# A graph network kernel: node rows sent in source order to runs of four slots, and summed from linear loads

## The reference

```python
def layer(x, conv):  return x + conv(relu(layernorm(x)))
# layer 0: Gaussian mixture; msg = einsum(xg[src], gauss(edge_attr)); mean over dst
# layer 1: SAGE mean, twice
h = relu(mean_over_dst(x[src]) @ W1_l + b1 + x @ W1_r)
out = mean_over_dst(h[src]) @ W2_l + b2 + h @ W2_r
# layer 2: spline convolutions on edge coordinates; summed over src (row = src, col = dst)
h = elu(spline_conv(ones)); h = elu(spline_conv(h)); h = elu(h @ w3 + b3)
t = h @ w4 + b4
new_pseudo = clip(pseudo + t[col] - t[row], 0, 1)
out = spline_conv(x, new_pseudo, conv_w)
# layer 3: SAGE with a sum instead of the mean, twice
```

## Time and profile before

| what | us |
|---|---|
| median of 3 runs | 15050.08 |
| fastest and slowest run | 15047.9, 15058.99 |
| the profiled execution's own time | 15074.62 |
| its span | 15072.8 |
| POOL busy in the span | 8971.3 |
| PE busy | 7096.2 |
| DVE busy | 5575.7 |
| ACT busy | 1755.8 |

### The profile page before, as it was taken

The page is one execution under the profiler, slowest core; times in us unless marked ns, Lnnn a source line. Parts: engine busy times, 40 slices in busy tenths (PEclk is TensorE's granted clock), DMA queues, the critical chain, the costliest instruction groups (busy, mean ns, idle before and its releaser), DMA issues. The chain is left out here.

```text
span 15072.8 us, 155974 instructions
## 1 busy us (share of the span) xinstructions
PE 7096.2 (47%) x32816; PEld 6021.4 (40%) x32819; DVE 5575.7 (37%) x11340; ACT 1755.8 (12%) x5296; POOL 8971.3 (60%) x9011
## 2 busy tenths in 40 slices
PE   5200455556665555455557775444444453334333
PEld 1100344446663333344446664433333343333332
DVE  8200344444445666333335554333233341111111
ACT  0000333322221111000010001111111110000000
POOL 0677566636665555555526665666666526664666
PEclk9555666655557777555555555555555555555555
DMA  7991111123331111211121112000111121112112
GB/s 271 139 106 13 53 67 67 64 70 91 89 86 34 42 41 40 26 30 31 30 13 12 12 12 15 12 12 12 21 23 23 24 34 12 12 12 12 13 13 14
DMA packets 790129, 641.91 MB, mean 43 GB/s; under 512 B 363646, under 2 KB 680304, under 8 KB 789814
## 3 DMA queue, kind: packets, MB, share of 16 engines
q1 hardware_dynamic: 466548, 303.70, 11.4%
q0 software_dynamic: 295168, 243.14, 9.1%
q10 hardware_dynamic: 28288, 93.72, 1.6%
HBM read 264.86 MB, written 386.20 MB: 43 GB/s over the span
## 5 line engine op out<-in xcount | busy, mean ns | idle before, releaser
L802 PE MATMUL ps<-got,oh 128*128 128x33 f32 x7040 | 1670.1, 400 | 2383.0 <-DVE oh L625 675.8
L802 PEld LDWEIGHTS ps<-got,oh 128*128 128x128 f32 x7040 | 1573.8, 327 | 2547.0 <-issue 2531.9
L765 POOL DMA_INDIRECT got<-q_table,idx x1760 | 1809.7, 1028 | 1186.1 <-DVE idx L807 657.2
L2144 POOL DMA_INDIRECT msg<-msg,idx x1792 | 1759.0, 982 | 1126.1 <-issue 524.4
L765 POOL DMA_INDIRECT got<-h_table,idx x1760 | 1719.1, 977 | 1116.8 <-issue 569.9
L1703 POOL DMA_INDIRECT cell<-rec,idx x880 | 921.6, 1047 | 609.4 <-ACT rec L1685 352.1
L348 POOL DMA_INDIRECT rec_r<-sc_rec,sc_idx x832 | 840.8, 1011 | 721.3 <-ACT sc_rec L339 423.2
L1367 POOL DMA_INDIRECT rec_d<-rec,idx x880 | 908.6, 1032 | 563.6 <-ACT rec L1307 310.5
L1969 POOL DMA_INDIRECT cell<-rec,idx x880 | 912.9, 1037 | 498.7 <-issue 270.8
L625 DVE TENSOR_TENSOR oh<-iota_f,rd 128x512 f32<-128x512 f32 x1105 | 759.7, 692 | 1025.1 <-DMA b<-in_L_gnn_b 498.2
L807 DVE CAST idx<-rd 128x4 int32 (+1 forms) x892 | 158.1, 178 | 2441.6 <-DMA msg<-msg,idx 634.8
(11 more groups left out here) (329 smaller groups left out, 13359.1 us busy)
## 6 DMA issues: line engine op xcount, KB each, us to landing
got<-rec_d SPq DMA_DIRECT2D x220, 416.0 KB
rec_d<-padd ACTq DMA_DIRECT2D x4, 11648.0 KB
rec_d<-padd ACTq DMA_DIRECT2D x4, 11232.0 KB
cin<-cell SPq DMA_DIRECT2D x224, 136.0 KB
msg<-msg,idx POOLq DMA_INDIRECT x1792
msg<-zpad SPq DMA_DIRECT2D x8, 3575.0 KB
got<-msg SPq DMA_DIRECT2D x220, 130.0 KB
cell<-rec,idx POOLq DMA_INDIRECT x1760
```

The costliest lines, as they stand in the source:

```text
L765: nc.gpsimd.indirect_dma_start(out=s["got"][:, n, g, :], out_offset=None, in_=table, in_offset=bass.IndirectOffsetOnAxis(ap=s["idx"][:, n, ...
L802: mm = nc.tensor.matmul(psum_rows[:, ds(at[g], W)], s["oh"][:, n, g, :], s["got"][:, n, g, 0:W], start=False, stop=False)
L2144: nc.gpsimd.indirect_dma_start(out=msgs, out_offset=bass.IndirectOffsetOnAxis(ap=idx[:, n, g:g + 1], axis=0), in_=msg[:, n, g, :], in_offs ...
```

## The change

The destination order is laid out anew. Inside a destination block edges are now sorted by source block as well, and the edges of one source block and one destination block take whole runs of RUN = 4 slots, the last one padded. That makes 944 tiles (236 batches, 59 turns of 4), of which the destination pass goes over 936 in turns of UBD = 6 batches instead of UB = 10. The "d" sort leaves the first phase; a new phase `place_by_runs` reads the source-ordered records back and makes the places from counts by block pairs.

With that, one source block's rows for a run are 4 x 128-lane picks. `send_runs` (four times) goes over 272 sets of 128 runs in source order: DVE compares the runs' local numbers with the lane (bf16), PE picks the rows in four bf16 matmuls from `planes`, in which a row's f32 values stand as three bf16 parts (HW = 100 values a slot; TW = 112 with t), ACT copies the result to `rec`, and POOL sends it with one indirect DMA, 128 runs of 800 B (896 B with t) to their places in run_h or run_t. `job_sum_runs` (four times) then loads 512 slots a batch linearly (SP), and PE adds them with twelve bf16 matmuls. Once, `source_runs` makes the runs' places and local numbers by way of DRAM, `job_send_ids` sends them in 236 indirect DMAs of 12 B beside `job_sum_out`, which now runs without a gather beside it, and `turn_ids` reads them back.

Tables: rec_d has 944 tiles. SP's fills in the scatter phase are now cell1 and msg1 alone; cell2 and msg2 are filled by ACT beside `job_sum_out`, waited for one by one. run_h and run_t are filled by ACT at the start of the source pass, sixteen issues in a row (`together=True`), and waited for at its end. h_table and q_table are gone, and so are most tick increments on PE, ACT and DVE. `to_cells` goes over 944 tiles.

```diff
-                    sort_sp(sp, srt["d"], "d", "d")
-                    sort_pe(pe, srt["d"], 50)
-                    parts, groups = 8, TILES_N // 4
+                    parts, groups = 8, TILES_D // 4
...
+        def blank_tables(eng, sem, tables, together=False):
+            parts, filled = 8, 0
+            for table, pad, tiles in tables:
+                groups = tiles // 2
...
+                for q in range(parts):
+                    t0, t1 = groups * q // parts, groups * (q + 1) // parts
+                    eng.dma_start(view[:, t0:t1, :], bcast(pad.unsqueeze(1), [P, t1 - t0, pad.shape[1]])).then_inc(sem, 16)
+                    filled += 16
+                    if not together:
+                        eng.wait_ge(sem, filled)
...
+        row_d = sb_in(early, "row_d", [P, TILES_N])
+        place_by_runs(row_d)
...
+                        blanks = blank_tables(act, s_blank, ((run_h, zpad[:, 0:HW], TILES_D), (run_t, zpad[:, 0:TW], TILES_D)), True)
                         act.wait_ge(s_const, 6)
                         act.wait_ge(s_ld[0], 16)
                         ramps(0, 0)
...
+        def send_runs(planes, W, runs):
+            RING = 4
...
+                                sp.dma_start(loc[:, u, :, :].rearrange("p b e -> p (b e)"),
+                                             bcast(loc_s[ds((i * UNROLL + u * HU) * RUN * P, HU * RUN * P)].unsqueeze(0),
+                                                   [P, HU * RUN * P])).then_inc(s_ld[u], 16)
...
+                                v.wait_ge(s_pick, k + 1)
+                                nc.vector.tensor_scalar(hot[:, m % RING, :], loc[:, u, m % HU, :], lane_c[:, 0:1], None,
+                                                        ALU.is_equal).then_inc(s_hot, 1)
...
+                                for g in range(RUN):
+                                    mm = nc.tensor.matmul(ps[:, m % RING, g * W:(g + 1) * W], hot[:, m % RING, g * P:(g + 1) * P],
+                                                          flat[:, ds(ids[m % HU] * W, W)], start=True, stop=True)
...
+                                act.wait_ge(s_pick, k + 1 + RING)
+                                nc.scalar.copy(rec[:, m, :].bitcast(BF16), ps[:, m % RING, 0:RUN * W]).then_inc(s_fill, 1)
...
+                                nc.gpsimd.indirect_dma_start(
+                                    out=out, out_offset=bass.IndirectOffsetOnAxis(ap=idx[:, u, m % HU:m % HU + 1], axis=0),
+                                    in_=rec[:, m, :], in_offset=None,
...
-        def job_sum_in_rows(c, table, width, acc, t_nm=None, new=None):
+        def job_sum_runs(c, runs, W, acc, planes=None, new=None):
...
+                        sp.wait_ge(free, i * R + n + 1)
+                        sp.dma_start(got[:, n, :, :], view[:, ds(i * STEP + n * G, G), :]).then_inc(loaded[n], 16)
...
                 for g in range(G):
-                    mm = nc.tensor.matmul(psum_rows[:, ds(at[g], W)], s["oh"][:, n, g, :], s["got"][:, n, g, 0:W],
-                                          start=False, stop=False)
+                    for q in range(3):
+                        mm = nc.tensor.matmul(psum_rows[:, ds(at[g], AW)], s["oh"][:, n, g, :], part_of[n][:, g, q * AW:(q + 1) * AW],
+                                              start=False, stop=False)
...
+                nc.vector.tensor_reduce(there[:, n % 2, :, :],
+                                        part_of[n][:, :, 3 * AW:3 * AW + 12].rearrange("p g (q f) -> p g f q", q=3)[:, :, 0:KD, :],
+                                        AX.X, ALU.add).then_inc(s_there, 1)
...
+                source_runs(pay, idx)
...
-                    run_sums(job_sum_in_rows(e, h_table, C + 1, acc_nm), job_sum_out(e, msg1, F1, acc_s[:, :]))
+                    run_sums(job_sum_out(e, msg1, F1, acc_s[:, :]),
+                             job_send_ids(pay, idx, sem_in(e, "sent"), ((cell2, pad2[:, :, :].rearrange("p u w -> p (u w)"), TC),
+                                                                        (msg2, zpad[:, 0:2 * (F2 + 1)], TILES_N)), sem_in(e, "blanked")),
+                             count=NI)
+                turn_ids()
...
+            send_runs(planes, HW, run_h)
+                run_sums(job_sum_runs(d, run_h, HW, acc_nm))
...
+            send_runs(planes_t, TW, run_t)
-                run_sums(job_sum_in_rows(d, q_table, QW, acc_nm, t_nm[:, :], new))
+                run_sums(job_sum_runs(d, run_t, TW, acc_nm, planes_t, new))
```

More of the change, by code:

```diff
@@ L49 @@
 ABANKS2 = -(-NB // PER_BANK2)
[L50 to L51 removed]
+MQ = 8
+MAPLEN = MQ * P
+assert max(TILES_C, TILES_N, TILES_D, SSETS) <= MAPLEN
 KS, KD = 5, 3
@@ L178, in halves_of, with count_bins @@
             return t.rearrange("p (h j) -> p h j", h=2)
-        def sort_dve(v, then, c, key, bins, blocks, tiles, row_out, tag):
+        def count_bins(v, c, key, bins):
             marks = c["marks"]
@@ L199, in sort_dve, with carry_bases @@
             then(nc.vector.tensor_scalar(c["first"][:, :], c["first"][:, :], float(P), None, ALU.mult))
-            then(nc.vector.scalar_tensor_tensor(out=seen[:, :], in0=seen[:, :], scalar=c["first"][:, 0:1], in1=total[:, :],
-                                                op0=ALU.add, op1=ALU.subtract))
+        def carry_bases(then, c):
+            seen, pos, lane = c["seen"], c["pos"], c["lane"]
             then(nc.vector.tensor_copy(pos[:, :], seen[:, :]))
@@ L205, in sort_dve, with keep_ranks @@
             nc.vector.tensor_copy(c["parts"][:, :], lane[:, :]).then_inc(c["carried"], 1)
+        def keep_ranks(v, then, c, key, bins, tiles, row_out):
+            marks, rank, pos, lane, half = c["marks"], c["rank"], c["pos"], c["lane"], c["rank"].shape[1] // 2
             def keep(b):
@@ L225, in sort_dve, with sum_columns, count_pe @@
                                                 op0=ALU.mult, op1=ALU.add))
+        def sum_columns(then, c):
+            total, seen = c["total"], c["seen"]
+            cols = total.shape[1]
+            then(nc.vector.tensor_copy(halves_of(total[:, :]), ps[:, 0:2, 0:cols // 2]))
+            then(nc.vector.tensor_tensor_scan(out=seen[:, :], data0=bcast(ones[:, 0:1], [P, cols]), data1=total[:, :],
+                                              initial=0.0, op0=ALU.mult, op1=ALU.add))
+        def sort_dve(v, then, c, key, bins, blocks, tiles, row_out, tag):
+            count_bins(v, c, key, bins)
+            total, seen = c["total"], c["seen"]
+            sum_columns(then, c)
+            nc.vector.tensor_scalar(c["diag"][:, :], ident[0:CELLS, 0:CELLS], seen[0:CELLS, EJ - 1:EJ], None,
+                                    ALU.mult).then_inc(c["spread"], 1)
+            v.wait_ge(c["summed"], 1)
+            sort_bases(then, c, ps[:, 2, 0:CELLS])
+            own_first(then, c)
+            then(nc.vector.scalar_tensor_tensor(out=seen[:, :], in0=seen[:, :], scalar=c["first"][:, 0:1], in1=total[:, :],
+                                                op0=ALU.add, op1=ALU.subtract))
+            carry_bases(then, c)
+            keep_ranks(v, then, c, key, bins, tiles, row_out)
             sort_map(then, c, tag, blocks)
-        def sort_pe(pe, c, bins):
-            marks, column, place = c["marks"], c["column"], c["place"]
+        def count_pe(pe, c, bins):
+            marks, half = c["marks"], c["rank"].shape[1] // 2
             for b in range(bins):
@@ L474, in _ @@
                     then(nc.vector.tensor_scalar(before[:, :], iota_f[:, :], lane_c[:, 0:1], None, ALU.is_gt))
[L475 to L478 removed]
+                    sort_consts(then, shared)
                     n_load = 16 * len(PARTS)
@@ L639, in layer_norm @@
+        def layer_norm(hT, kept=None, planes=None):
             with ExitStack() as c:
@@ L841, in dve_end @@
+                v.wait_ge(s_there, k + 1)
+                nc.vector.tensor_tensor(rd[:, ds(t, G), NEWP:NEWP + KD], here[:, n % 2, :, :], there[:, n % 2, :, :],
+                                        ALU.subtract).then_inc(s_new, 1)
+                v.wait_ge(s_new, 2 * k + 2)
+                v.wait_ge(s["summed"], k + 1 + R)
+                nc.vector.sem_inc(free, 1)
             def dve_end(v):
-                if t_nm is not None:
-                    for _ in rank_turn(v, new, s_rank, NI - 1):
+                if planes is not None:
+                    for _ in rank_turn(v, new, s_rank, NID - 1):
@@ L1037, in _ @@
                         chunk(NCH - 1, False)
+                        v.wait_ge(s_qn, NCH + 1)
+                        split_planes(then, planes, q_nm[:, :, :], rest[:, :, :], t_nm and t_nm.rearrange("p (b f) -> p b f", f=4))
         def post_rows(acc, mean, bias=None):
```

826 lines of the change are left out of this document (560 added, 266 removed).

## The result

The changed kernel takes 14590.21 us in the median (14581.76 to 14602.44), against 15054.53 for the kernel before in the same comparison: a ratio of 0.9688, 95% interval 0.9676 to 0.9700. Its profiled span is 14599.4 us, 473 less than before.

What follows compares the result with a forecast made beforehand. No engine was taken as busy throughout; stages behind barriers each had their own limit. Stage terms, savings from removed gathers against added sorts, fills, sends and sums, gave +168 on 15050, about 15,218 us; eight in ten from 14,620 to 15,560.

Steps and rivals of the forecast that it cites:

- job_sum_runs: Linear sums, four times: 2.1 us a batch, 496 us for each plain one, bounds 400 and 590.
- Twelve pairs ... 12 x 0.12: Linear sums: twelve weight loads and matmuls a batch at 0.12 us each, plus 0.29 and 0.33, making 2.06 us.
- The hold of ACT in the source pass: Source pass start: sixteen fill issues block ACT before its first ramps, +360 us, bounds 190 and 390.
- rival 1: Source pass: the fills don't hold ACT, issues go out 0.4 us apart; 14,858 us in all, chance 0.17.
- The sum of the messages: Layer 1, spline sum running alone: 2.55 us a batch, 560 us, with POOL scatters and moved fills beside it.
- The sends: send_runs, four times: 272 steps at POOL's 1.37 us plus 10, 380 us each, bounds 355 and 440.
- rival 3: Sends: DVE compares hold up POOL, steps over 1.5 us, windows over 420; +294, 15,510; chance 0.23 with rival 4.
- The ranking sum: Layer 1's second pass: DVE-bound, 20 us a turn including 2 us of added operations, 1180 us, bounds 1090 and 1475.
- Rival 4: Ranking pass keeps its 25 us turn because its stalls are its own: +295, 15,513; chance 0.23 with rival 3.
- Sorts: First phase: one of the two block sorts leaves, -121 us.
- turn_ids: Layer 1: 34,816 pieces of 12 B read back at 600 a microsecond, and nine transposes, 75 us.
- Rival 2: Linear sums at 1.75 us a batch, cheaper sends and ranking turn: 420 less, 14,800; chance 0.20 including mixes with rival 1.

Runs made afterwards that it cites:

- e3: The changed kernel with the two inner loops of the linear sums exchanged, so consecutive matmuls never share weights: 14594.15 us.
- e4: The changed kernel with a register computation ahead of each of a batch's twelve matmuls in the linear sums, loading sixteen numbers instead of four: 15765.46 us.
- e8: The changed kernel with run_h rows of 102 values a slot instead of 100, so fill rows of 408 B instead of 400: 14613.21 us.
- e1: The changed kernel with the fills of cell2 and msg2 put back on SP in the scatter phase: 14531.45 us.
- e2: e1 with the fills of run_h and run_t also on SP in the scatter phase, and ACT's sixteen issues dropped: 14306.52 us.
- e9: e2 with POOL's sends of ids in job_send_ids paced, each waiting until one more batch is summed: 14083.6 us, ratio 0.9376.
- e11: e9 with rings of eight PSUM banks and eight compare buffers in send_runs instead of four: 14081.94 us, ratio 0.9355.
- e6: e2 with POOL, ahead of each fourth send of ids, waiting for the group of four before the last and incrementing tick: 14369.86 us.

## Why the prediction was wrong, step by step

**The sign** turns on one term. job_sum_runs was put at 2.1 us a batch and takes 281/236 = 1.19. The step that failed is "Twelve pairs ... 12 x 0.12": it took the spacing of matmuls in the earlier trace rows for the price of a matmul and its weight load. It was the price of the register computation ahead of each (e3, e4), of which the change needs four a batch and not twelve. The trace of before had the hint: L1786 and L1787 share their weights and are 0.12 apart all the same, as far as two with new weights, and each has a register computation of its own (880 and 880). Twelve matmuls and the pause behind them are 0.62 + 0.44 = 1.06 in the middle of a turn, where 1.44 + 0.62 = 2.06 was put, so the pause was nearly right; over the stage it is 1.19. With 281 us for each plain sum, the forecast would have been 3 x 215 = 645 lower, -477 instead of +168, and the result was -473. That exact match is luck, since other terms were off as well and cancelled:

- The hold of ACT in the source pass was right as a mechanism (rival 1 is out) and mis-sized: 237 us instead of 385, of which the stage lost 224. The price a row of run_h was taken at the upper end, 77 ns, and that of run_t at 37; they are 38 and 28 (18.0 and 13.2 us for the 472 rows an engine of one transfer). The 34 ns in the expectation for e8 is misread.
- The sum of the messages was put at 560, with "236 POOL scatters and the moved fills lie beside it" at nothing. It took 809. The fills added nothing to that (e1). The scatters cost about 266 us, by their being issued without idle time, which makes PE's increments late (e2 against e9); with e9's 549 us the 560 for the work itself was right.
- The sends: some 430 us each instead of 380, in the stated bounds. Both recorded signs of rival 3 came, a step above 1.5 us and a window above 420, and yet rival 3 is out: the compares don't lengthen POOL's steps, and the rest are gaps behind PE's late increments. By the Trainium skill ("SBUF — State Buffer", "SBUF: two separate sides") a DVE operation in a two-port mode would shut out GpSimd's descriptor writing; the trace doesn't show it here, since POOL's pitch beside the compares is 1.28 us as in the earlier trace rows.
- The ranking sum took 1036 us, 17.6 a turn instead of 20. The wait for the gathered sums and the stalls of the earlier trace rows are gone, together with POOL's gathers, and DVE is busy for 13.6 us a turn (801.90/59) where it was 13.1, so the added operations were put too high at 2 us. Rival 4 is out. The removal of the ticks in its chain wasn't tried alone.
- Sorts (-117 for -121), place_by_runs (156 for 175), destination pass and messages (+64 for +88), to_cells (+71 for +98), source_runs (168 for 200): within 35 us each. turn_ids, put at 75, takes 25, so its small pieces are read back faster than the 600 a microsecond that was taken.

Rival 2 named the right term, the linear sums, and put it at 1.75 a batch, still far over 1.19, and with too small a share of the chance. The lower bound of 400 us a sum was worked out by hiding the ids, never by asking what the 0.12 was made of; so the range ended 30 us too high.

By the rule of 512 B for line rate in the Trainium skill ("DMA: Bandwidth & Descriptors", "Specifications") the term would have been about 600. The stage lost 224; rows of 400 and 448 B cost 38 and 28 ns, those of 520 B in the earlier trace rows 88, so the trace speaks against size as what decides, as before.

## What to carry to other kernels

Before a spacing in a timeline is used as a price, ask which instruction makes it: the engine's work, or the register computation or number load that its queue needs ahead of it, and whether the new code needs one for each operation or one for several. When POOL issues a long row of indirect DMAs beside other work, give it a wait that follows that work; here this and fills moved under a phase that bears them took the changed kernel from 14590 to 14084 us (ratio to the kernel before 0.9376 instead of 0.9688). A deeper ring doesn't do it (e11). Sixteen issues of 7,552 rows each held ACT for 237 us though it waited for none of them, so such fills belong on an engine that has nothing else to do.

## What the runs showed of the hardware that I had not expected

- With a register computation ahead of each, bf16 matmuls of 33 columns with their weight loads come 0.12 us apart at the clock of 0.50 (e4, twelve in 1.50 us). With four computations for twelve the mean is 0.04 us with weights that repeat (the change) and 0.05 with weights that don't (e3); those without a computation of their own follow 0.03 us apart.
- A load of numbers into PE's registers takes 0.33 us for four and 1.10 us for sixteen (e4), and in these sums the matmuls wait for it.
- While POOL issues indirect DMAs with 0.30 us between them, PE's increment is seen some 18 us late in the median batch (e1, e2, e6), DVE's is not, and a stage of 549 us takes 815. Three DMAs in 4.9 us don't do this. In the send of e11 that was shown PE's increments are seen singly, one in some 6 us, while POOL's row lasts, and many at once when it stops.
- A fill of 400 B rows costs 38 ns a row and engine at the start of the source pass, 48 beside the scatters (e2), and one of 408 B rows 28% more than 38 (e8).
